# A second wait ahead of GpSimd's gathers in a two-layer graph network: the freed chunk's sums, and then TensorE's next scores or edges

## What is computed

```python
# layer 0
q, k, v = h @ Wq.T + bq, h @ Wk.T + bk, h @ Wv.T + bv
e = concatenate([edge_attr, cos(abs(node_vec[src] - edge_weight) * time_w + time_b)]) @ We.T
alpha = sum(q[dst] * (k[src] + e)) / sqrt(128)
alpha = softmax of alpha over the edges of each dst
m = segment_sum((v[src] + e) * alpha, dst)
x = layernorm(x + tanh(h + tanh(h @ A.T + m + b_ac)))
# layer 1
edge_new = relu(concatenate([x[src], x[dst]]) @ We1 + be1) @ We2 + be2
agg = segment_sum(edge_new, dst)
x = layernorm(x + x + mlp(concatenate([x, agg])))
```

## Time and profile before

| | before |
|---|---|
| median of 3 runs | 5643.19 us (5636.46 to 5644.07) |
| the profiled execution: time, span | 5636.47 us, 5634.6 us |
| PE / PEld busy | 4098.4 us (73%) / 3750.1 us (67%) |
| GpSimd (POOL) busy | 3027.8 us (54%) |
| VectorE (DVE) / ScalarE (ACT) busy | 2252.4 us (40%) / 1728.9 us (31%) |
| L641, gathers of layer 0 | 1563 of 953 ns |
| L1394, gathers of layer 1 | 1563 of 943 ns |
| mean granted TensorE clock | 0.660 |

### The profile page before, as it was taken

One profiled execution on the slowest core, in us unless ns is written; L12 is line 12 of the kernel. 1 busy time (PEld: TensorE's weight loads), 2 busy tenths in 40 slices (PEclk: granted clock), 3 DMA queues, 4 the chain that ended last, 5 costly groups with the idle time before them and its releaser, 6 DMA issues. The chain is left out here.

```text
span 5634.6 us, 82995 instructions
## 1 busy us (share of the span) xinstructions
PE 4098.4 (73%) x24167; PEld 3750.1 (67%) x24167; DVE 2252.4 (40%) x5558; ACT 1728.9 (31%) x2766; POOL 3027.8 (54%) x3202
## 2 busy tenths in 40 slices
PE   5777777777777777777776477777777777777778
PEld 2666676676666777666775366677666666766676
DVE  2545455454545445454555322222222222222223
ACT  2444444444434444444444211111111111111113
POOL 5355555555555555555551566666666666666660
PEclk7877777777777777777778655555555555555556
DMA  4222222222222222222222211111111111111111
GB/s 121 60 50 51 51 53 51 51 53 50 52 50 52 52 52 50 51 51 51 52 53 68 68 48 48 47 48 48 47 47 48 47 47 48 47 47 47 48 47 31
DMA packets 398442, 292.85 MB, mean 52 GB/s; under 512 B 266467, under 2 KB 341755, under 8 KB 398300
## 3 DMA queue, kind: packets, MB, share of 16 engines
q0 software_dynamic: 100032, 205.87, 15.0%
q1 hardware_dynamic: 289948, 81.55, 6.6%
q10 hardware_dynamic: 8386, 4.57, 0.3%
HBM read 271.33 MB, written 20.32 MB: 52 GB/s over the span
## 5 line engine op out<-in xcount | busy, mean ns | idle before, releaser
L641 POOL DMA_INDIRECT he<-h_table,src_i x1563 | 1490.3, 953 | 1410.6 <-PE p_sum L706 903.4
L1394 POOL DMA_INDIRECT msg<-p_table,src x1563 | 1474.5, 943 | 900.3 <-issue 447.4
L1434 PE MATMUL p_sum<-hot,msg 128*128 128x80 f32 x3136 | 737.6, 416 | 226.5 <-issue 225.4
L1434 PEld LDWEIGHTS p_sum<-hot,msg 128*128 128x128 f32 x3136 | 706.7, 331 | 207.6 <-issue 207.2
L1422 PE MATMUL p_edge<-r_win,hotT 80*128 80x128 f32 x3136 | 742.8, 431 | 117.1 <-ACT hotT L1463 86.7
L1463 ACT ACTIVATE hotT<-p_hot 80x512 f32<-80x512 bf16 x392 | 216.0, 588 | 1991.9 <-DMA qk_table<-qk 1255.7
L1422 PEld LDWEIGHTS p_edge<-r_win,hotT 80*128 80x128 f32 x3136 | 684.1, 330 | 158.2 <-ACT hotT L1463 108.9
L682 PEld LDWEIGHTS p_score<-qk_win,heT 128*128 128x128 f32 x3136 | 641.6, 271 | 0.0
L865 DVE SCALAR_TENSOR_TENSOR score<-other,p_score 128x320 f32<-128x320 bf16 x392 | 190.2, 488 | 1100.3 <-remote 1058.7
L682 PE MATMUL p_score<-qk_win,heT 128*128 128x80 f32 x3136 | 621.3, 339 | 0.0
L1507 DVE TENSOR_TENSOR msg<-msg,p_edge 128x512 f32<-128x512 f32 x392 | 262.5, 684 | 785.0 <-remote 680.9
(11 more groups left out here) (184 smaller groups left out, 5612.3 us busy)
## 6 DMA issues: line engine op xcount, KB each, us to landing
feat<-in_edge_attr_dram SPq DMA_DIRECT2D x196, 128.0 KB
he<-h_table,src_i POOLq DMA_INDIRECT x1563
msg<-p_table,src POOLq DMA_INDIRECT x1563
qk_win<-qk_table SPq DMA_DIRECT2D x196, 40.0 KB
qk_two<-qk_table SPq DMA_DIRECT2D x392, 20.0 KB
r_win<-r_table SPq DMA_DIRECT2D x196, 40.0 KB
qk_table<-qk SPq DMA_DIRECT2D x13, 512.0 KB
h_table<-h_rows ACTq DMA_DIRECT2D x13, 258.0 KB, 4.1
```

What stands on the lines that cost most here:

```text
L641: e.indirect_dma_start(out=he[u][:, j, 0:ROW], out_offset=None, in_=h_table[:, :], in_offset=bass.IndirectOffsetOnAxis(ap=src_i[u][:, j:j ...
L1394: e.indirect_dma_start(out=msg[u][:, j, :], out_offset=None, in_=p_table[:, :], in_offset=bass.IndirectOffsetOnAxis(ap=src_i[u][:, j:j + 1 ...
L1434: e.matmul(p_sum[:, 0, :], msg[u][:, j, :], hot[u][:, j, :], start=(j == 0), stop=(j == J - 1))
```

## The change

GpSimd waits for one semaphore more ahead of each chunk's eight gathers. In layer 0 it is `score_full[1]`, the second half of the scores, at the count c - 3, which is reached when the scores of chunk c - 4 have ended; in TensorE's order these are the scores that follow the sums of chunk c - 7. In layer 1 it is `edge_full[1]` at the count c - 4, the edges of chunk c - 5, which in TensorE's order follow the sums of chunk c - 7 directly. For the first chunks, where the count is not positive, nothing is waited for. The wait for the sums stays. In the changed file, lines behind the first insertion are 3 higher, and those behind the second 6.

```diff
@@ -637,6 +637,9 @@
                             again(e, sum_full, val(e, count(c) - SLOTS + 1))
                             e.sem_inc(passed, 1)
 
+                            again(e, score_full[1], val(e, count(c) - SLOTS + 4))
+                            e.sem_inc(passed, 1)
+
                             for j in range(SKIP if is_last(c) else 0, J):
                                 e.indirect_dma_start(
                                     out=he[u][:, j, 0:ROW], out_offset=None, in_=h_table[:, :],
@@ -1390,6 +1393,9 @@
                             again(e, sum_full, val(e, count(c) - SLOTS + 1))
                             e.sem_inc(passed, 1)
 
+                            again(e, edge_full[1], val(e, count(c) - SLOTS + 3))
+                            e.sem_inc(passed, 1)
+
                             for j in range(SKIP if is_last(c) else 0, J):
                                 e.indirect_dma_start(
                                     out=msg[u][:, j, :], out_offset=None, in_=p_table[:, :],
```

## The result

| | before | after |
|---|---|---|
| median of 4 runs, side by side | 5641.66 us (5636.46 to 5644.07) | 5699.69 us (5692.72 to 5705.61) |
| profiled execution: time, span | 5636.47 us, 5634.6 us | 5694.81 us, 5693.0 us |
| ratio | | 1.0104, interval 1.0086 to 1.0121 |

The change makes the kernel 58 us slower. The prediction said 6260 us, 617 us slower: the sign was right and 5699.69 lies in the range of 5640 to 6450, but the loss was put at ten times what it is. The time lies between the rival "no effect", 5643 us, and the leaky rival, 5790 us, and a little nearer to the former; which mechanism is at work is for the traces to say.

The account below looks back on a forecast made before the run. Bound: the chunk period, since TensorE's signals are seen late while GpSimd issues gathers. Layer 0 17.74 against 14.74 us a chunk, +567 us; layer 1 +53 us; 5636.5 + 567 + 53 = 6256, about 6260 us; range 5640 to 6450 us.

Parts of the forecast that it names:

- rival "no effect": Gathers are not the cause, TensorE itself is late; the added wait moves only work with slack: 5643 us, chance 0.06.
- leaky rival: Layer 0: the tops' signal gets through during the burst, ring 15.2 us a chunk; about 5790 us in all, chance 0.14.
- Layer 0, the gain: Scores finish in a stretch without gathers: their 7.9 us of lateness vanish and the sums begin with an open window.
- Layer 0, where the lateness goes: The closed window now falls on the transpose of the next tops (L690), the chain's next link, prompt before.
- second term of the ring: Layer 0's period: from the first gather to the opening of the window, when the tops are read, 11.88 us.
- third term: Layer 0's period: from the tops' end to the scores' end, 5.68 us at the mean granted clock 0.77.
- first term: Layer 0's period: from the scores' end to the first gather, 0.81 us.
- burst with a pause: Layer 0: one burst in nine pauses over 1 us between two gathers; those chunks were put at 12.7 us.
- +53 us put: Layer 1: edges' signal falls into the closed window, 12.43 us a chunk against 12.15, +0.28 x 189.
- bursts never join: Layer 1: the change keeps bursts from running into one another, each starting about 0.8 us behind a read of the edges.
- main case: Ring with late tops: 6260 us, own range 5950 to 6450 us, chance 0.66.
- layer 1's floor: Layer 1: if the edges get through, the burst itself is the floor, 9.97 us a chunk, -412 us.

Follow-up runs that it names:

- g1: Kernel before without the gathers after the first seven chunks of each layer, in a group with late signals: 4161.9 us, ratio 0.724.
- groups A and E: Two sets of runs, each on one chip, with prompt signals; the kernel before takes 4330.79 and 4332.01 us there.
- h1: Kernel before with the added wait in layer 0 alone, late signals: 5857.85 us, ratio 1.025.
- h2: Kernel before with the added wait in layer 1 alone, late signals: 5732.98 us, ratio 1.0018.
- group D: Set of runs on one chip with late signals; the kernel before takes 5722.64 us there.
- i2: Kernel before with layer 0's burst split, six gathers behind the sums and two behind the scores, prompt signals: 4333.84 us, ratio 1.0003.
- e1: Changed kernel without the new wait of layer 1, prompt signals: 4333.97 us, ratio 1.0016.
- g2: Kernel before with each burst halved, four gathers behind the sums, four behind scores (layer 0) or edges (layer 1), late signals: 5422.8 us, ratio 0.9433.
- e5: Kernel before with each burst halved, four gathers behind the sums, four behind scores (layer 0) or edges (layer 1), prompt signals: 4330.45 us, ratio 0.9993.
- e4: Kernel before without the gathers after the first seven chunks of each layer, prompt signals: 4062.91 us, ratio 0.938.
- f4: Kernel before with gathers fetching a third of each row in layer 0, an eighth in layer 1, after seven chunks, late signals: 5621.02 us, ratio 1.001.
- h3_l0_quarters: Kernel before with layer 0's burst in quarters, two gathers each behind sums, spread of tops, scores and last turn, late signals: 5439.09 us, ratio 0.9497.

## Why the prediction was right, and where it was wrong

**What bounds the kernel: right.** The period of layer 0 is set by a signal that is read late, and in the groups with late signals it is late with the gathers alone: without them 1586 of 5748 us are gone, with the same matmuls (g1). In groups A and E the same gathers hold nothing, so they are needed for the lateness and not enough for it. The Trainium skill, "SBUF — State Buffer", section "Who interferes with whom", says that a DMA never contends with a compute engine. Read as "gathers can't slow the other engines", it does not agree with the 4161.9 against 5747.78 us; the page speaks of the ports of that memory, and no run here shows what part of the chip the gathers hold up. By that rule the change would have given 5643 us, and the interval of the ratio, 1.0086 to 1.0121, excludes that.

**Layer 0, the gain: right.** The scores are read on time (lateness 5.04 to 0.04 us) and the sums stop creeping (344 to 16 us).

**Layer 0, where the lateness goes: right.** It falls on the tops (0.04 to 3.34 us), and h1 and h2 show that layer 0 carries the loss.

**Layer 0, the second term of the ring, 11.88 us from the first gather to the reading of the tops: wrong, and this is the step that failed.** Measured is 7.1 us in the usual chunks (mean and median), from 3.7 to 11.6 (5% and 95% of them). Two things were wrong in it. First, I took the tops' end to be 5.0 us into the burst, and it is 3.5. The 2.44 us that I gave the turns, from 1516.58 to 1519.02, held a pause of TensorE of 0.91 us in the kernel before, and without it turns and sums take 4.26 us from the scores' end to the tops', not 5.8. The kernel before, TensorE in the earlier trace rows's chunk, and VectorE for what follows:

```profile
1514.57 0.57 PE L682 MATMUL p_score<-qk_win,heT 128*128 128x80 f32 x4
...
1517.49 0.66 PE L659 MATMUL p_turn<-ident,rest 128*128 128x128 f32 x4 [0.91 <-issue]
```

```profile
1516.34 0.82 DVE L909 TENSOR_TENSOR qk<-score,p_turn 128x640 f32<-128x640 f32 x1
1517.25 0.49 DVE L865 SCALAR_TENSOR_TENSOR score<-other,p_score 128x320 f32<-128x320 bf16 x1
```

Second, I took the window as shut for the tops until 2.2 us behind the last gather. In the usual chunk above they are read 7.11 us in, with a gather still to come, and in 126 of 147 usual bursts before the last gather has ended. The rule that I had from the scores holds for the scores (150 of 154) and did not carry over to a signal that ends 3 us earlier in the burst: the hold is leaky there. Two rows had spoken for that, and it deserved more than 0.14. One is the earlier trace rows, with sums that were read 8.7 us into a run. The other is the first half of the scores in the earlier trace rows, which I had taken as getting through: its last matmul ends at 1514.57 + 0.57 = 1515.14, and it is read at 1517.25. VectorE was at work until 1516.34 + 0.82 = 1517.16, which hid that the signal was late: the update of its semaphore stands in the trace at 1517.10, 2.0 us behind the matmul and with four gathers still to come. Why the scores are held to the burst's end and the tops are not stays open. The value from the leaky rival, 0.81 + 8.73 + 5.68 = 15.2 us, is near the measured mean period, 15.18 us, by luck: its 8.73 us were 7.1, and the two other terms were larger than put, as the next point shows.

**Layer 0, the third term, 5.68 us from the tops to the scores' end: too small.** Measured is 7.3 us. I gave the stretch the mean granted clock of the stage, 0.77, but it comes just behind TensorE's idle time, and its own mean is 0.59, as the window from 900 to 908 shows, with 0.55. Nor were the 6.88 us of the earlier trace rows the half clock's: the last four records there take 0.57 us, as at the full clock in the earlier trace rows, where in the changed kernel's chunk they take 0.98. The mean clock of a stage is not the clock of the stretch behind a stop. The first term, 0.81 us, is right as a median; its mean is 1.5 us, since the scores' own signal is still late by up to 4.9 us in some chunks.

**The burst with a pause: 12.7 us put, 10.0 us measured** (median 9.0). Behind the pause the tops pass at once, and then the clock stays up.

The sum of layer 0 again, with what was measured: eight chunks in nine take 15.89 us (about 1.5 + 7.1 + 7.3), not 18.37, and the ninth 10.0, not 12.7: (8 x 2.48 + 2.7) / 9 = 2.50 us a chunk too much, times 189 = 473 us of the 567. What is left, 94 us, is nearly what the periods give, (15.18 - 14.71) x 189 = 89 us.

**Layer 1: +53 us put, next to nothing measured.** The periods are 12.14 us in both; from the first to the last sums layer 1 is 7 us longer, and group D has +10 us (h2). The statement "bursts never join" is wrong: in 51 places of the changed kernel's trace a burst still starts within 0.5 us of the end of the one ahead (in 52 before), since the edges' signal is there by then. The ring that I had put in place of the pairs is therefore not the one that runs. TensorE's pauses within the sums of layer 1, 353.7 us from 3300 to 5500 us, are gone, and 206.5 us within the edges have come.

**Not foreseen: the ends of the loops.** The gathers of chunks 4 to 6 now wait too, so the first run of gathers is 32 long and not 56, and the first sums end at 164.0 instead of 185.3 us: -21 us. The stretch between the loops is 11 us shorter (213.1 to 202.2), the tail 5 us (73.4 to 68.2). All together: 89 + 0 to 7 - 21 - 11 - 5 = 52 to 59 us, against 58 measured.

**The range.** Its lower bound of the main case, 5950 us, does not follow from its own terms: layer 1's floor alone, -412 in place of +53, takes 6260 to 5800 us. The stated range of 5640 to 6450 held the result by its rivals, not by the main case.

**The signs that I had named.** Seen: L868 within 1 us of the scores, the idle time before the gathers put down to the scores' matmul (L685), less creeping. Not as said: VectorE's wait for the tops is late by 3.3 us in the median and not 5 to 7; GpSimd's busy share of layer 0 is 1258.80 / 2540 = 50%, where 43% was said; bursts in layer 1 join.

**What stays open.** Why signals are late in some groups and prompt in others, through which part of the chip the gathers hold them, and how the hold grows with the number of gathers beside an event: the run with six and two gathers (i2) fell in a group with prompt signals. One rival is untested. Every execution here was recorded by the profiler, and the traces of the late groups hold far fewer updates of semaphores than those of the same kernel in a prompt group: 37,473 (h1) against 92,419 (e1), 33,393 (g2) against 92,047 (e5), but without gathers 46,818 (g1) against 49,095 (e4). A gather's landing raises its semaphore by 16 (`then_inc(rows_in[u], 16)`), in steps of one. So the updates, or their recording, may be what is congested where signals are late, which would also fit that the bytes don't matter (f4 has as many gathers); no run without recording, and none with as many gathers and fewer updates, tests it.

**A version better than both.** Where signals are late, splitting the burst gives 5422.8 us (g2_split, -5.7%, interval -5.9 to -5.4%) and 5439.09 us (h3_l0_quarters, -5.0%, -5.2 to -4.9%); where they are prompt it costs nothing (e5_split, 0.9993, 0.9982 to 1.0004). It keeps the scores nearly clear of lateness (0.25 and 0.12 us), as the change does, and leaves half as many gathers beside the tops.

## What to carry to other kernels

Where a table of waits has an engine waiting for "remote" or for a result whose matmuls have ended, measure the lateness for every link of the chain, and then look at what runs at that time on engines that have nothing to do with it. When a burst that disturbs a chain is moved, it disturbs the next link, so split it or lay it beside links with slack, and price the new link by how late signals were that ended at the same place in a burst, not by how late the last ones were. Price the work behind a stop at the clock of such stretches, and compare two kernels only beside one another in the same group of runs.

## What the runs showed of the hardware that was not expected

- One program, the kernel before, takes 4331 us (39 runs in two groups) or 5619 to 5748 us (four groups, 47 runs): a third more, each within half a per cent of its group's median but for one run of 7135 us.
- In the late groups the indirect DMAs that GpSimd issues (0.95 us each with 0.30 us between) delay what the others see of TensorE in layer 0 by 3 to 5 us in the median (scores before, tops after), up to 9.4 us (h1), and TensorE pauses between matmuls by up to 2.6 us; the signals of VectorE and ScalarE are not late; the bytes don't matter (205.87 or 53.09 MB, 5618.55 and 5621.02 us). In the prompt groups the same DMAs delay nothing.
- One burst in nine has a pause of 1.3 us between two gathers, and an event behind it is seen at once (974.47, 0.13 us late; median 0.11 us over 19 such bursts).
- Signals that were held come out in their order, 0.06 us apart (median, kernel before), not each some time after its own event.
- After 3.6 us of idling TensorE's granted clock, 1.00 until then, is 0.55 over the next 8 us.
